# A GNN and expert network on one core: identity products on TensorE ahead of four of its waits

## The reference, cut to what matters

```python
x = x + _L0_gnn_ref(_layernorm(x, axis=-1), edge_index, L0_gnn_W, L0_gnn_a_left, L0_gnn_a_right)
x = x + _L0_ffn_ref(_layernorm(x, axis=-1)[None], L0_ffn_gate_w, L0_ffn_gate_b, L0_ffn_w1, L0_ffn_w2, L0_ffn_w3)[0]
x = x + _L1_gnn_ref(_layernorm(x, axis=-1), edge_index, edge_attr_8, batch0, L1_gnn_W1, ...)
x = x + _L1_ffn_ref(_layernorm(x, axis=-1)[None], L1_ffn_attention_mask, L1_ffn_wr, ...)[0]
```

```python
logits = jnp.einsum('bsd,de->bse', x, gate_w) + gate_b
probs = jax.nn.softmax(logits, axis=-1)
top_probs, top_idx = jax.lax.top_k(probs, 2)
top_probs = top_probs / jnp.sum(top_probs, axis=-1, keepdims=True)
...
h1 = jnp.einsum('bsd,edh->bseh', x, w1)
h2 = jnp.einsum('bsd,edh->bseh', x, w2)
hidden = jax.nn.silu(h1) * h2
expert_out = jnp.einsum('bseh,eho->bseo', hidden, w3)
return jnp.einsum('bseo,bse->bso', expert_out, dispatch)
```

## Time and profile before

| | us |
|---|---|
| median of 3 executions | 3875.2 |
| lowest and highest | 3874.25 and 3875.74 |
| the profiled execution's own time | 3887.48 |
| its span, first to last instruction | 3885.8 |
| TensorE busy in the span | 3477.1 (89%) |
| VectorE busy | 2881.9 (74%) |
| ScalarE busy | 2384.7 (61%) |
| mean granted TensorE clock | 0.960 |

### The profile page before, as it was taken

How to read it: one execution, slowest core, us unless ns; L and a number is a source line. 1 busy time by engine, 2 the same in 40 slices (tenths; PEclk the granted TensorE clock), 3 DMA queues, 4 the chain that set the end, 5 groups by cost and what they waited for, 6 DMA issues and landing times. The chain is left out here.

```text
span 3885.8 us, 69748 instructions
## 1 busy us (share of the span) xinstructions
PE 3477.1 (89%) x27387; PEld 2708.3 (70%) x27388; DVE 2881.9 (74%) x4412; ACT 2384.7 (61%) x3738; POOL 231.3 (6%) x230
## 2 busy tenths in 40 slices
PE   6998979888889888888947999699999999999799
PEld 4555546666666666666647998588878887888577
DVE  6999989999999999999853222565556555655494
ACT  4778778888888888888810110266656665444432
POOL 1000000000000000000002444100000000000010
PEclk8999989999999999999958999899999999999899
DMA  4423211111114121111176886333223331333100
GB/s 135 160 98 130 97 57 58 65 53 70 53 61 195 53 71 53 64 59 53 37 232 203 238 233 185 92 122 113 104 72 128 108 108 69 140 116 117 41 23 34
DMA packets 146755, 398.39 MB, mean 103 GB/s; under 512 B 20419, under 2 KB 92380, under 8 KB 128380
## 3 DMA queue, kind: packets, MB, share of 16 engines
q1 hardware_dynamic: 124950, 353.45, 26.1%
q0 software_dynamic: 15552, 36.16, 3.9%
q10 hardware_dynamic: 5926, 4.26, 0.5%
HBM read 331.83 MB, written 61.99 MB: 101 GB/s over the span
## 5 line engine op out<-in xcount | busy, mean ns | idle before, releaser
L913 ACT ACTIVATE hd_probsT<-hd_psT 128x768 f32<-128x768 f32 (+1 forms) x800 | 648.6, 836 | 186.1 <-PE hd_psT L996 185.3
L996 PE MATMUL hd_psT<-ident,hd_scores 128*128 128x128 f32 (+1 forms) x5000 | 739.0, 286 | 14.3 <-ACT hd_scores L904 14.3
L944 DVE SCALAR_TENSOR_TENSOR hd_scores<-el_heads,hx 128x3136 f32<-128x3136 f32 x200 | 695.6, 3478 | 0.9 <-PE hd_psT L996 0.9
L948 DVE CUSTOM_DVE_ANT_0 hd_scores<-hd_scores,mask_heads 128x3136 f32<-128x3136 f32 x200 | 684.0, 3420 | 8.6
L1010 PE MATMUL hd_psO<-hd_probsT,hx 128*32 128x128 f32 (+1 forms) x10000 | 582.5, 286 | 98.7 <-ACT hd_probsT L913 97.8
L996 PEld LDWEIGHTS hd_psT<-ident,hd_scores 128*128 128x128 f32 (+1 forms) x5000 | 545.2, 143 | 168.1 <-issue 166.2
L904 ACT ACTIVATE hd_scores<-hd_scores,hd_negmax 128x1664 f32<-128x1664 f32 (+1 forms) x400 | 640.9, 1602 | 8.2 <-DVE hd_negmax L948 8.2
L1417 PE MATMUL ly_psO<-hx_a,ly_probsT 128*128 128x256 f32 x2500 | 584.0, 381 | 0.0
L1375 ACT ACTIVATE ly_probsT<-ly_psT 128x768 f32<-128x768 f32 (+1 forms) x300 | 249.3, 831 | 470.1 <-PE ly_psT L1406 469.9
L1010 PEld LDWEIGHTS hd_psO<-hd_probsT,hx 128*32 128x32 f32 (+1 forms) x10000 | 322.5, 110 | 297.5 <-ACT hd_probsT L913 174.0
L1417 PEld LDWEIGHTS ly_psO<-hx_a,ly_probsT 128*128 128x128 f32 x2500 | 454.0, 189 | 71.4 <-issue 16.6
(11 more groups left out here) (327 smaller groups left out, 3900.0 us busy)
## 6 DMA issues: line engine op xcount, KB each, us to landing
ly_mask<-mask_dram SPq DMA_DIRECT2D x75, 1568.0 KB, 6.5
mask_heads<-mask_dram SPq DMA_DIRECT2D x48, 1568.0 KB, 6.8
moe_w<-in_L_ffn_w SPq DMA_DIRECT2D x144, 512.0 KB, 5.2
mask_dram<-logc SPq DMA_DIRECT2D x200, 196.0 KB, 1.9
el_heads<-el_dram POOLq DMA_DIRECT2D x4, 1568.0 KB, 18.8
el_heads<-el_slope_dram POOLq DMA_DIRECT2D x4, 1568.0 KB, 23.2
el_heads<-el_dram SPq DMA_DIRECT2D x4, 1568.0 KB, 10.3
el_heads<-el_slope_dram SPq DMA_DIRECT2D x4, 1568.0 KB, 14.2
```

The costliest lines, as they stand in the source:

```text
L913: nc.scalar.activation(pT[:, gi % 2, 0:w], psT[gi % 2][:, 0:w], ACT.Copy).then_inc(s_ev, 1)
L944: nc.vector.scalar_tensor_tensor(sc[:, c, :], el[:, h, 0, :], hx[:, b, o:o + 1], el[:, h, 1, :], ALU.subtract, ALU.min).then_inc(s_lk, 1)
L948: nc.vector.tensor_tensor_reduce(out=sc[:, c, :], in0=sc[:, c, :], in1=mask[:, B % 2, :], scale=1.0, scalar=3.0e38, op0=ALU.add, op1=ALU.m ...
L996: last = nc.tensor.transpose(psT[gi % 2][0:r, t * P:(t + 1) * P], sc[:, u % 3, c0:c0 + r], g["ident"][:, :])
```

## The change

A helper issues n products of the 128x128 identity with itself into a PSUM bank that nothing reads. It waits for nothing. It is called in five places: 24 products at the start of TensorE's list in the gating layernorm, one after each block's gating product there (23 times, from b = 2 on), 24 in the router ahead of the 100 products of the slot table, 16 in the expert phase ahead of the first transpose, and 24 in the projection ahead of the first transpose. Four PSUM banks are allocated for it, one in each phase.

```diff
+def keep_busy(nc, g, out, n):
+
+    for _ in range(n):
+        nc.tensor.matmul(out[:, 0:P], g["ident"][:, :], g["ident"][:, :], start=True, stop=True)
...
@@ node_phase
             s_gw = sem("s_gate_w")
+            fill = ctx.enter_context(nc.psum_tensor(f"{name}_filler", [P, 512], F32))
...
             if gate is not None:
+                keep_busy(nc, g, fill, 24)
                 pe.wait_ge(s_gw, 16)
             for b in range(NB):
...
                 if gate is not None and b >= 2:
                     gating(b - 2)
+                    keep_busy(nc, g, fill, 1)
@@ node_project_phase
+        fill = ctx.enter_context(nc.psum_tensor("np_filler", [P, 512], F32))
...
+            keep_busy(nc, g, fill, 24)
             for b in range(NB + 2):
                 if b < NB:
                     transpose_x(b)
@@ router_phase
+        fill = ctx.enter_context(nc.psum_tensor("rt_filler", [P, 512], F32))
...
                     last.then_inc(s_wa, 1)
+            keep_busy(nc, g, fill, 24)
             for i in range(2):
                 pe.wait_ge(s_sel, i + 1)
@@ moe_phase
+        fill = ctx.enter_context(nc.psum_tensor("moe_filler", [P, 512], F32))
...
+            keep_busy(nc, g, fill, 16)
             transpose_x(0)
```

## The result

The changed kernel takes 3893.26 us (median of five executions, 3886.81 to 3895.74), the kernel before, beside it, 3875.2 (five, 3874.25 to 3886.76). The ratio is 1.0038 with a 95% interval of 1.0020 to 1.0055: slower by 14.7 us, between 7.8 and 21.3. The two medians alone stand 18.1 apart. The forecast of +3.4 and its range up to 3883.5 were both too low.

The account below looks back on a forecast made before the run. TensorE, at 1.2 GHz in the gating loop, was taken to set the gating layernorm's end. The terms 5.4 − 0.3 − 1.4 − 0.3 = +3.4 us gave a median of 3878.6 us, range 3871.5 to 3883.5.

Parts of the forecast that it names:

- Part 2, 23 fillers in the loop: Gating loop: fillers lengthen TensorE's path to the phase's end, partly offset by a faster gate bias load; +5.4 us.
- 9.4: Gating loop: us added by the 23 fillers at 0.39 to 0.43 each, from a span of 9.0 to 9.9.
- +5.4: Router's start: net us by which the logits start later because of the loop's fillers, with ends 5.0 and 9.9.
- Part 1: Ahead of the gating layernorm: 24 fillers hide under the wait for loads and statistics and change nothing.
- Part 4: Expert phase: 16 fillers speed the first tile's 32 products; −1.4 us, carried to the end, ends −0.2 and −1.8.
- What bounds the kernel: Gating layernorm: TensorE, at 1.2 GHz, sets the phase's end, with SyncE 0.92 us behind.
- the logits start near 2011.9 + 3.5: Router's start: the gate bias, issued at 2011.9, lands some 3.5 us later instead of 7.5, no longer queued behind stores.
- No rise in the loop: Gating loop: one filler behind six other pairs leaves TensorE's clock at PEclk 0.50.
- rival B: Router's start: gate bias lands as late after issue as before, so the loop's 9.4 to 9.9 passes on; chance 0.09.
- Parts 3 and 5: Router and projection: 24 fillers each might keep the clock full until the work starts; −0.3 us each, ends 0 and −2.0.
- The sum: Whole kernel: 5.4 − 0.3 − 1.4 − 0.3 = +3.4 us.
- 12.3 us as the cost of profiling: Whole kernel: the profiled execution's 12.3 us above the median of 3875.2 taken as profiling cost that both kernels pay.

Follow-up runs that it names:

- e2: The changed kernel without the 23 fillers in the gating loop, the other four places kept; median 3877.93 us, ratio 1.0007 to the kernel before.
- e6: The kernel before with only the 24 fillers of 128 columns ahead of the gating layernorm added; profiled span 3895.7 us.
- e7: The kernel before with only 6 products of 512 columns added ahead of the gating layernorm; profiled span 3883.7 us.
- e8: The changed kernel with ScalarE's loads of the second and third layer's attention weights moved behind the router's exponential; single time 3888.75 us.
- e5: The kernel before with only the loop's fillers added, each one product of 512 columns instead of 128; median 3887.01 us, ratio 1.0031.
- e4: The changed kernel run again unaltered; median 3887.96 us, ratio 1.0037 to the kernel before.
- e9: The changed kernel without fillers in or ahead of the gating layernorm, 36 instead of 24 in router and projection; median 3875.16 us, ratio 1.0001.
- e10: The kernel before run again without an edit; 3871.95 us profiled.

## Why the prediction was wrong

What bounds the phase and what the clock does were as predicted. What failed first is "Part 2, 23 fillers in the loop", the sum's largest term: the fillers cost 12.2 and not 9.4, and the wait for ScalarE behind the bias was left out, so that +5.4 came out as +10.4. Then the "nothing" of Part 1, which was +1 to +2, and in Part 4 the step that the first tile's gain "is carried to the end", which no run shows.

- **What bounds the kernel**: right. TensorE set the end of the gating layernorm, and all that the loop's fillers took came out at its end.
- **Part 1, "nothing"**: wrong by 1.4 in the changed kernel, 0.8 to 2.1 over all runs with these fillers. I asked only whether TensorE's fillers end before TensorE is needed, which they do. I hadn't asked what else in the phase's first microseconds they touch. e2 (48.5), e6 (47.5) and e7 (48.4) show it against 46.4 to 46.7.
- **Part 2, "9.4"**: 12.2. The price of a pair was taken from the loop's average pace (0.197) and from the narrow pairs (0.215), and the sum took a value between them. With the filler in it the six pairs that were there took longer too, the four gating pairs above all: 6 × (0.214 − 0.197) = 0.10 a pass. The upper end, 8 × 0.215 − 1.18 = 0.54, could have been worked out from the same rows; a loop at the pace of its new kind of pair, not "old pass plus two pairs".
- **Part 2, "the logits start near 2011.9 + 3.5"**: the landing was right (3.95, −3.6). The next wait was missed: ScalarE's DMA issues ahead of the exponential, +1.8, taken back in e8 by moving six of the nine. The prediction named what else queues on ScalarE only as a cause of a slow landing (rival B). So half of what the earlier bias gave was lost one step later. "+5.4" came out as 12.2 − 3.6 + 1.8 = +10.4, above its own dear end of 9.9.
- **No rise in the loop**: right, 0.50 throughout. The Trainium skill's advice (TensorE: Matmul & The Clock Gate, "Why this matters for your kernels") to keep TensorE continuously busy is, by the profile's busy time, again contradicted: 36 us fully busy, fillers and all, at 0.50. Only with the 512-column filler of e5 did the clock rise in this loop.
- **Parts 3 and 5, −0.3 each**: the question of the gap was right and came out at the poor end: nothing in the changed kernel's own profile. In e4, where the gap is 3.97 instead of 4.27, the way from the slot table to the experts is 21.3; the runs without fillers there have 21.4 to 22.4, so this may be spread. e9 shows what a shorter gap gives. The projection had no gain: 50.4 to 52.3 with 24 fillers (e2, e4, e8, changed kernel), 50.0 to 51.6 without. Its first transposes come at 11.9 to 12.2 in three of the four against 11.4 to 11.5 in most runs without them, but e7 has 11.8 without; why, no run told apart.
- **Part 4, −1.4**: right for the first tile. The first 32 products take 3.81 in each run with these fillers and 5.2 to 6.6 without them, 1.4 to 2.8 less. That it "is carried to the end" is not shown: the eleventh tile's transposes come 67.3 to 69.1 after the phase's start with these fillers and 68.0 to 72.1 without, 67.9 and 68.0 in the pair of e4 and e10, and the expert phases of that pair are 380.7 and 380.6. The waits for gathered rows from the sixth tile on can take the gain back.
- **The sum**: 1.4 + 12.2 − 3.6 + 1.8 − 1.7, and 0 to 1 in the projection, gives +10 to +11, and about +12 if the first tile's 1.7 is not carried; the fair pair has +12.7. The executions together have +14.7, between 7.8 and 21.3, so they fit either, but what may lie above +12.7 has no cause here. The range ended at +8.3, because its upper end was rival B alone. It had no term for a new wait behind the bias, nor for B's kind of mishap together with a dearer filler.
- **12.3 us as the cost of profiling**: wrong, as shown above, and without effect on the median.

## What to carry to other kernels

Filler work belongs where the engine is idle until the very moment its work comes: 16 products that ended at the first transpose took 1.7 us off the work behind them (though not, as far as the runs show, off the phase), 24 that ended 4 us ahead won nothing, and one in a loop that bounds its phase cost 0.53 us a pass, or 0.34 as the wide one that brought the full clock (1.52 against 1.18). When a wait gets shorter, look up what every other engine did under it; here DMA issues on ScalarE took half of the gain. And compare phases, not totals, where one phase has a spread of its own.

## What I had not expected of the hardware

- With fillers in it the weight load and product pairs of the loop took 0.214 us at PEclk 0.50, while the same transposes and gating products took 0.197 on average without them; the difference is in the four gating pairs, 0.72 a pass before and 0.86 with a filler behind them.
- Work of TensorE with no DMA of its own goes with a DMA issue of SyncE that takes 1.3 to 1.7 us instead of 0.52, with an instruction packet in the queue at that time.
- The same program's expert phase varied from 380.6 to 392.1 us between two executions (403.3 in e6, whose code there is unchanged), in stretches of tiles that wait for gathered rows; all other parts of these two stayed within 1.5 us of each other. In e6 such tiles follow one another for over 100 us; two of them in TensorE's timeline:

```profile
2107.01 0.44 PE L1820 MATMUL moe_ps_xT<-ident,moe_x 128*128 128x128 f32 x2 [1.34 <-DMA moe_x<-xn_dram,slot_token]
...
2122.58 0.44 PE L1820 MATMUL moe_ps_xT<-ident,moe_x 128*128 128x128 f32 x2 [1.30 <-DMA moe_x<-xn_dram,slot_token]
```
